# Gates of a Mamba layer's kernel by the silu table in two visits a chunk, and smaller pieces of matrix work between the scan's steps

## The chip, the cores and the metric

One core of a Trainium2 chip runs the program. The metric is the device time of one execution in microseconds (us); the times shown are the median, the lowest and the highest of several executions. A core has a matrix engine (TensorE, "PE" in the profile, with its weight loads as "PEld"), a vector engine (VectorE, "DVE"), a scalar engine (ScalarE, "ACT"), a general one (GpSimd, "POOL") and a queue engine that issues transfers (SyncE, "SP"). Each engine takes its own instructions in order; they meet at semaphores.

## What is computed

The input is x of 4 sequences, 2048 rows each, 256 wide. Two residual layers follow, in float32:

```python
x = x + mamba(layernorm(x));  x = x + ffn(layernorm(x))

# mamba: D_INNER = 512, 16 states
xp, res = split(x @ W_in.T)
xc = silu(conv4(xp) + conv_b)                      # 4 taps along the sequence
B, C, dt = split(xc @ W_x.T)                       # 16, 16 and 1 columns
dt = softplus(dt @ W_dt.T + b_dt)
h = exp(A * dt) * h + dt * B * xc                  # a recurrence over the rows, 512 x 16 states
y = silu(einsum(h, C) + D * xc + res)
return y @ W_out.T

# ffn: ternary weights, 1024 hidden
h = silu(w1(x) * s1) * (w2(x) * s2)
h = gelu(h1(h) * t1);  h = gelu(h2(h) * t2);  return w3(h) * s3
```

## The kernel before

The first part of the program runs over 32 chunks of 256 rows (T = 256). Per chunk it makes the recurrence for 16 states, one state a step, n = 0 to 15, and between these steps all engines do pieces of other stages on other chunks. While the scan works on chunk c, stage `norm` is at chunk c+2, `front` (projection, convolution, gate of the convolution, dt, B and C) at c+1, `post` (gate of y, output projection, residual) at c-1, and `mlp` (first two layers of the feed-forward part, up to the product with h1) at c-1, c-2 and c-3. A second part, from about 2222 us on, makes the other two layers of the feed-forward part over 16 blocks. The change leaves that part as it is.

A step of the scan, on every engine:
- ACT makes two decays (L1028, exp of a chunk's dt times A, 128x510, half of the channels each) into one of three banks of PSUM, so it can be at most three decays ahead of the scan, and copies the last column of an earlier state (`carry`, L1000).
- POOL makes `ub` (L767, L768), two buffers.
- DVE runs two scans (L1165) for state n+1, then adds state n's turned rows, times C, to `acc` (L1178, twice).
- PE turns the state with transposes (L1453), four for each half q of the rows, once the scans are done and DVE has added the same half of the state before. DVE's two additions for n come after the scans for n+1, so PE has about one step for them.

The places of everything else are a table written out by hand: `PE_AT`, `DVE_AT`, `ACT_AT`, `POOL_AT`, `SP_AT`. PE and ACT have 32 places a chunk (place 2n after the first half of step n, place 2n+1 after the second), DVE has 48, POOL and SP 16. A place of `mlp` of 32 and over on PE and ACT lies in a later chunk's body (place 54 is place 22, step 11, one body later). Results of PE's jobs go to three work banks (RA = 3) handed out in the order of the jobs; a job's first piece waits until the bank's last reader is done, and all that PE has behind it waits too.

Gates before: silu(v) is v times (0.5 tanh(0.5 v) + 0.5), as tanh lies in one table set with exp.
- Convolution: ACT copies the bank to `xc` with its bias (L908, four), takes tanh (L915) and a scaled copy (L917) over 128x1024, POOL multiplies (L724).
- y: ACT tanh (L956) and scaled copy (L958) of `acc`, POOL multiplies (L777) into `g`.
- Feed-forward: eight blocks of 128x256 in four pairs. ACT takes tanh of uu (L983), DVE makes (tanh + 1) times uu (L1142, once a pair, frees the bank), then times gg (L1150, twice a pair); ACT rounds to `act_high` (L990), POOL makes the rest (L791), PE multiplies with h1 (L1441).
- softplus: ACT copies dt to `z` (L927, four), takes Abs (L933), Relu (L935) and exp (L937) of 128x1024, then the logarithm (L860).
- Logarithms of softplus and of both layer norms come together in `with_logs`, between two table loads (L865, L876).

Of the kernel before, what the change touches and what calls it, by code (L numbers as in the profile page):

```python
# [31 lines left out]
P = 128  # L32
# [7 lines left out]
def program(nc, x, w_in, conv_w, conv_b, w_x, w_dt, b_dt, a_log, d_skip, w_out,  # L40
# [26 lines left out]
    with ExitStack() as ctx:  # L67
# [11 lines left out]
        half_s1 = sb("half_s1", [P, KH])  # L79
        gate_scale = sb("gate_scale", [P, KH])  # L80
# [74 lines left out]
        tanh1 = sb("tanh1", [P, 2, 2, T], where=a_only)  # L155
        wide1 = sb("wide1", [P, 2, 2, T], where=a_only)
# [65 lines left out]
        scales_ready = sem("scales_ready")  # L222
# [33 lines left out]
        gate_step = sem("gate_step")  # L256
# [11 lines left out]
        tanh_ready = sem("tanh_ready")  # L268
# [9 lines left out]
        def after(eng, s, value):  # L278

            if not (isinstance(value, int) and value <= 0):  # L280
# [6 lines left out]
            norm={25: ('xn',), 27: ('xp0',), 31: ('xp1',)},  # L287
            front={1: ('conv0.a',), 3: ('conv0.b',), 5: ('conv1.a', 'conv1.b'), 14: ('ssm',), 15: ('dtc',), 21: ('acc0',), 25: ('acc1',)},
            post={8: ('gT0',), 11: ('gT1',), 16: ('out.a',), 18: ('out.b',)},
            mlp={28: ('yn',), 39: ('uu0.a',), 40: ('uu0.b',), 45: ('gg0.a', 'gg0.b'), 46: ('uu1.a', 'uu1.b'), 47: ('gg1.a', 'gg1.b'), 49: ('uu2.a', 'uu2.b'), 51: ('gg2.a', 'gg2.b'), 53: ('uu3.a', 'uu3.b'), 56: ('gg3.a',), 57: ('gg3.b',), 63: ('h0.a', 'h0.b'), 65: ('h0.c',), 71: ('h0.d',), 73: ('h1.a', 'h1.b'), 76: ('h1.c', 'h1.d'), 87: ('h2.a', 'h2.b'), 88: ('h2.c',), 89: ('h2.d',), 92: ('h3.a',), 93: ('h3.b',), 95: ('h3.c', 'h3.d')})  # L290
        DVE_AT = dict(low2=44, up=(68, 71, 79, 85), gated=(69, 72, 79, 86))
        ACT_AT = dict(sums=8, x1=22, sums2=25, logs=26, xn=29, xp=(2, 4), conv=(10, 10), silu=13, ssm=17, z=20, soft=21, acc=(26, 30), gate=5, gT=14, high2=32, tanh=(46, 47, 48, 50, 55, 56, 56, 59), high=(49, 53, 58, 61), z_out=(75, 80, 93, 101), a_dt=31)
        POOL_AT = dict(gate=4, silu=7, normalize=14, normalize2=14, dt=14, u=15, low=(25, 27, 29, 31))
        SP_AT = dict(x=0, x1=7, res=15, write_b=7, b=(9, 12, 2, 4), z_out=(35, 41, 46, 47))

        LAST_PIECE = {"uu0": "b", "uu1": "b", "uu2": "b", "uu3": "b", "gg0": "b", "gg1": "b", "gg2": "b", "gg3": "b",
                      "conv0": "b", "conv1": "b", "out": "b", "h0": "d", "h1": "d", "h2": "d", "h3": "d"}
        MLP_BODIES = 4
        PE_STEPS, DVE_STEPS, ACT_STEPS = 2 * NS, 3 * NS, 2 * NS
# [1294 lines left out]
```

## Time and profile before

| what | us |
|---|---|
| median of 3 executions | 2822.73 |
| lowest, highest | 2822.26, 2822.75 |
| the profiled execution, its time | 2821.17 |
| its span, first to last instruction | 2819.5 |
| PE busy | 2623.1 (93%) |
| DVE busy | 2349.9 (83%) |
| ACT busy | 1944.3 (69%) |
| POOL busy | 1840.3 (65%) |

The mean granted clock of TensorE was 0.983 of full speed. Shares of the whole span mix two parts: DVE and POOL are busy almost only in the first. So the table of busy time by stage, the interval from one chunk to the next, and the starts of neighbouring instructions in the timeline say more than the page's shares. In a timeline the duration shown runs a little into the next instruction on the same engine; the distance between two starts is what an instruction takes of its engine's time.

### The profile page before, as it was taken

Reading aid. Unit: us, or ns where it says so; the run is one execution under the profiler, and the core shown is the slowest. Engines: PE = TensorE matmul, PEld = TensorE weight load, DVE = VectorE, ACT = ScalarE, POOL = GpSimd, SP = SyncE. Lnnn points to the kernel's source line nnn. Section 1 sums busy time; section 2 is a strip of 40 time slices with the busy share of each in tenths; the row PEclk is TensorE's granted clock in tenths of the full one; section 3 lists DMA queues with packets and bytes.
Section 4 is the critical chain, followed back from the end, with each engine's and each line's share of the span. In section 5 each row is a group of like instructions: output and inputs, shape, how many; then the busy total and the mean of one; then the engine's idle time right before and its main releaser. Section 6 shows DMA issues by size and latency. Waiting matters only on the chain.

```text
span 2819.5 us, 49137 instructions
## 1 busy us (share of the span) xinstructions
PE 2623.1 (93%) x17154; PEld 2337.7 (83%) x17154; DVE 2349.9 (83%) x3053; ACT 1944.3 (69%) x4040; POOL 1840.3 (65%) x1546
## 2 busy tenths in 40 slices
PE   6678999999999999999999999999978999999998
PEld 4557888888888888888888888888868888888887
DVE  4899999999999999999999999999985455555554
ACT  6888888888888888888888888888866322222221
POOL 3788888888888888888888888888874000000000
PEclk8789999999999999999999999999989999999999
DMA  6111122121221221112112121121132322222211
GB/s 227 42 42 46 57 63 67 57 70 60 61 68 58 64 62 58 58 60 70 57 62 68 57 72 58 61 65 58 54 128 68 114 81 90 83 83 90 90 61 31
DMA packets 130154, 198.78 MB, mean 71 GB/s; under 512 B 16368, under 2 KB 93296, under 8 KB 129904
## 3 DMA queue, kind: packets, MB, share of 16 engines
q1 hardware_dynamic: 129904, 195.57, 21.9%
q8 instruction: 141, 2.31, 0.4%
q14 instruction: 109, 0.89, 0.1%
HBM read 144.68 MB, written 50.86 MB: 69 GB/s over the span
## 4 chain that ended last, share of the span: by engine, by line
PE 49%; ACT 21%; DVE 15%; issue 9%; DMA 1%; POOL 0%; DVEq 0%; ACTq 0%; SPq 0%; POOLq 0%
PE banks L1479 17%; PE banks L1441 9%; DVE h L1165 8%; PE banks L1453 6%; DVE acc L1178 5%; ACT banks L1028 5%; PE banks L1491 4%; PE banks L1357 4%; PE banks L1341 4%; PE banks L1379 2%; ACT act_high L990 2%; PE banks L1427 2%; ACT g L927 1%; ACT L865 1%; ACT L876 1%
## 5 line engine op out<-in xcount | busy, mean ns | idle before, releaser
L1165 DVE TENSOR_TENSOR_SCAN h<-banks,ub 128x512 f32<-128x512 f32 x1024 | 1203.2, 1209 | 75.5 <-ACT banks L1028 61.3
L768 POOL TENSOR_TENSOR ub<-u,b_row 128x1020 f32<-128x1020 f32 x512 | 1215.4, 2374 | 0.1
L1028 ACT ACTIVATE banks<-dt,neg_a 128x510 f32<-128x510 f32 x1024 | 695.0, 684 | 59.0 <-DVE h L1165 59.0
L1178 DVE SCALAR_TENSOR_TENSOR acc<-banks,c_tok,acc 128x512 f32<-128x512 f32 x1024 | 712.6, 738 | 9.6 <-issue 5.1
L1453 PE MATMUL banks<-ident,h 128*128 128x128 f32 x4096 | 580.5, 276 | 71.8 <-DVE acc L1178 69.6
L1453 PEld LDWEIGHTS banks<-ident,h 128*128 128x128 f32 x4096 | 478.4, 143 | 119.4 <-DVE h L1165 68.0
L1441 PE MATMUL banks<-act_high,h_rounded 128*128 128x256 f32 x2048 | 525.0, 294 | 13.3 <-ACT z_out L805 9.0
L1441 PE MATMUL banks<-act_low,h_rounded 128*128 128x256 f32 x2048 | 499.3, 282 | 0.0
L1441 PEld LDWEIGHTS banks<-act_high,h_rounded 128*128 128x128 f32 x2048 | 389.7, 190 | 14.2 <-ACT z_out L805 9.3
L1479 PE MATMUL banks<-act_high,h_rounded 128*128 128x512 f32 x1024 | 398.9, 390 | 0.0
L1479 PE MATMUL banks<-act_low,h_rounded 128*128 128x512 f32 x1024 | 398.9, 390 | 0.0
L1441 PEld LDWEIGHTS banks<-act_low,h_rounded 128*128 128x128 f32 x2048 | 391.0, 191 | 0.0
L1066 ACT ACTIVATE wide<-banks,scales 128x512 f32<-128x512 f32 x128 | 88.1, 688 | 408.2 <-PE banks L1479 408.2
L1427 PE MATMUL banks<-xT_high,w_rounded 128*128 128x256 f32 x1024 | 277.3, 302 | 23.1 <-ACT acc L805 18.8
L1241 DVE CAST act_high<-wide 128x512 fp32r<-128x512 f32 x128 | 54.1, 423 | 263.9 <-PE banks L1491 236.2
L1427 PE MATMUL banks<-xT_low,w_rounded 128*128 128x256 f32 x1024 | 254.7, 280 | 0.0
L1357 PE MATMUL banks<-xp,conv_diag 128*128 128x256 f32 x1024 | 238.0, 380 | 0.0
L791 POOL TENSOR_TENSOR act_low<-wide,act_high 128x512 fp32r<-128x512 f32 x128 | 164.3, 1284 | 110.5 <-ACT act_high L990 110.5
L767 POOL TENSOR_TENSOR ub<-b_u,enter 128x4 f32<-128x4 f32 x512 | 104.6, 204 | 195.8 <-DVE h L1165 187.1
L1479 PEld LDWEIGHTS banks<-act_high,h_rounded 128*128 128x128 f32 x1024 | 192.2, 188 | 40.3 <-issue 0.3
L1479 PEld LDWEIGHTS banks<-act_low,h_rounded 128*128 128x128 f32 x1024 | 192.3, 188 | 39.5
L1427 PEld LDWEIGHTS banks<-xT_high,w_rounded 128*128 128x128 f32 x1024 | 193.0, 188 | 36.2 <-ACT acc L805 24.4
(126 smaller groups left out, 4287.6 us busy)
## 6 DMA issues: line engine op xcount, KB each, us to landing
b_row<-b_scratch SPq DMA_DIRECT2D x128, 512.0 KB, 4.3
z_scratch<-z_out SPq DMA_DIRECT2D x128, 256.0 KB, 3.5
zl<-z_scratch SPq DMA_DIRECT2D x32, 1024.0 KB, 8.0
x_sb<-in_x SPq DMA_DIRECT2D x32, 256.0 KB, 3.1
x_res<-in_x SPq DMA_DIRECT2D x32, 256.0 KB, 4.9
h_full<-in_h SPq DMA_DIRECT2D x2, 4096.0 KB, 16.5
x_scratch<-x_sb SPq DMA_DIRECT2D x32, 256.0 KB, 2.2
xr<-x_scratch SPq DMA_DIRECT2D x16, 512.0 KB, 4.8
```

The lines of the kernel that those rows point to most:

```text
L768: nc.gpsimd.tensor_tensor(ub[:, n % 2, :, 1:], u[:, :, 1:], b_row[:, n // QUARTER % 2, n % QUARTER:n % QUARTER + 1, 1:].to_broadcast([P, E ...
L791: nc.gpsimd.tensor_tensor(act1_low[:, c % 2, 2 * p:2 * p + 2], wide1[:, p % 2], act1_high[:, c % 2, 2 * p:2 * p + 2].bitcast(F32), ALU.sub ...
L1028: nc.scalar.activation(decay_half(k)[:, :, 1:], dt[:, par, 2 * i:2 * i + 2, 1:], ACT.Exp, scale=neg_a[:, n:n + 1]).then_inc(decay_ready, 1)
L1165: nc.vector.tensor_tensor_scan(h[:, n % 2, 2 * i:2 * i + 2].rearrange("p e t -> p (e t)"), banks[:, k % DECAYS, :], ub[:, n % 2, 2 * i:2 * ...
L1178: nc.vector.scalar_tensor_tensor(out=acc[:, par, q], in0=turned[q], scalar=c_tok[:, par, q, n:n + 1], in1=acc[:, par, q], op0=ALU.mult, op ...
L1341: last = nc.tensor.matmul(into[:, i * T:(i + 1) * T], w_in_sb[:, d, e * P:(e + 1) * P], xnT[:, d], start=(d == 0), stop=(d == KD - 1))
L1357: last = nc.tensor.matmul(into[:, i * T:(i + 1) * T], conv_diag[:, e, tap], xp[:, e, tap:tap + T], start=(tap == 0), stop=(tap == TAPS - 1))
L1427: last = nc.tensor.matmul(into[:, i * T:(i + 1) * T], weights[:, d, o * P:(o + 1) * P], rows[:, d], start=(d == 0 and rows is xT_high), st ...
L1441: last = nc.tensor.matmul(into[:, i * T:(i + 1) * T], rounded["h1"][:, k, o * P:(o + 1) * P], rows[:, c % 2, k], start=(k == 0 and rows is ...
L1453: last = nc.tensor.transpose(turned[q][:, e * P:(e + 1) * P], h[:, n % 2, e, q * P:(q + 1) * P], ident[:])
L1479: last = nc.tensor.matmul(into, rounded["h2"][:, k, o * P:(o + 1) * P], part[:, k], start=(k + i == 0), stop=(k == KH - 1 and i == 1))
L1491: last = nc.tensor.matmul(into[:, i * DIM:(i + 1) * DIM], part[:, k, q * P:(q + 1) * P], rounded["w3"][:, k], start=(k == 0 and part is ac ...
```

## The change

- Silu of the convolution, of y and of the feed-forward gate is taken by the silu table, straight out of the banks for convolution and uu, in place for `acc`. POOL's two products, DVE's L1142, the scaled copies and tanh go. DVE's other product (two a pair) stays, with s2 itself as its scale; `silu1` has room for all four pairs.
- ACT visits the silu set twice a chunk: at place 10 for the four convolution blocks of the next chunk and the gate of y of the chunk before, at place 26 for all eight uu blocks. Each visit loads the silu set first and the set with log and exp after. The logarithms need no loads of their own any more, and `with_logs` goes.
- softplus takes Abs and Relu out of the bank, four instructions of 128x256 each, in place of four copies and one instruction each.
- PE's pieces are cut finer (convolution in quarters, `ssm`, `xp`, `acc`, `out` in parts), and the places of nearly everything are new.
- The gelu rows for the second part's first block come one body later.

```diff
         PE_AT = dict(
-            front={1: ('conv0.a',), 3: ('conv0.b',), 5: ('conv1.a', 'conv1.b'), 14: ('ssm',), 15: ('dtc',), 21: ('acc0',), 25: ('acc1',)},
+            front={0: ('conv0.a',), 2: ('conv0.b', 'conv0.c'), 3: ('conv0.d', 'conv1.a'), 5: ('conv1.b', 'conv1.c', 'conv1.d'), 11: ('ssm.a', 'ssm.b'), 13: ('dtc',), 23: ('acc0.a', 'acc0.b', 'acc0.c'), 25: ('acc1.a', 'acc1.b'), 26: ('acc1.c',)},
+            post={12: ('gT0',), 13: ('gT1',), 14: ('out.a',), 15: ('out.b',), 17: ('out.c', 'out.d')},
+            mlp={32: ('yn',), 51: ('uu0.a',), 52: ('uu0.b', 'uu1.a'), 53: ('uu1.b',), 54: ('uu2.a', 'uu2.b', 'uu3.a', 'uu3.b', 'gg0.a'), 57: ('gg0.b', 'gg1.a'), 58: ('gg1.b',), 59: ('gg2.a', 'gg2.b', 'gg3.a'), 61: ('gg3.b',), 71: ('h0.a', 'h0.b', 'h0.c', 'h0.d'), 72: ('h1.a',), 73: ('h1.b',), 74: ('h1.c', 'h1.d'), 79: ('h2.a',), 80: ('h2.b', 'h2.c', 'h2.d'), 81: ('h3.a',), 83: ('h3.b', 'h3.c', 'h3.d')})
-        DVE_AT = dict(low2=44, up=(68, 71, 79, 85), gated=(69, 72, 79, 86))
+        DVE_AT = dict(low2=56, gated=(87, 88, 89, 93))
...
+            def silu_conv(c):
+                for j in range(2):
+                    wait_full(act, f"conv{j}", c)
+                    for i in range(2):
+                        e = 2 * j + i
+                        last = nc.scalar.activation(xc[:, e], bank(f"conv{j}", c)[:, i * T:(i + 1) * T], ACT.Silu, bias=conv_b_sb[:, e:e + 1])
+                    last.then_inc(freed(f"conv{j}", c), 1)
...
+                nc.scalar.activation(acc[:, c % 2], acc[:, c % 2], ACT.Silu).then_inc(g_ready, 1)
...
+                for i in range(2):
+                    o = 2 * p + i
+                    last = nc.scalar.activation(silu1[:, p, i], bank(f"uu{p}", c)[:, i * T:(i + 1) * T], ACT.Silu, scale=scales[:, 0, o:o + 1])
+                last.then_inc(freed(f"uu{p}", c), 1)
...
-                    if s == DVE_AT["up"][p]:
-                        pair = tanh1[:, p % 2].rearrange("p i t -> p (i t)")
-                        nc.vector.scalar_tensor_tensor(out=pair, in0=pair, scalar=1.0, in1=bank(f"uu{p}", c),
-                                                       op0=ALU.add, op1=ALU.mult).then_inc(freed(f"uu{p}", c), 1)
```

ACT around step 13 of a chunk, before (carry and decays are the scan's own; sig, log_var and rstd the logarithms and roots):

```order
L1000 ACTIVATE carry<-h,keep 128x4
L1028 ACTIVATE banks<-dt,neg_a 128x2x255
L990 ACTIVATE act_high<-wide 128x512
L865 ACT_TABLE_LOAD
L860 ACTIVATE sig<-sig 128x1024
L824 ACTIVATE log_var<-row_square,eps 128x2
L852 ACTIVATE log_var<-row_square,eps 128x2
L828 ACTIVATE rstd<-log_var 128x2
L856 ACTIVATE rstd<-log_var 128x2
L876 ACT_TABLE_LOAD
L805 ACTIVATE acc<-banks 128x512
L1028 ACTIVATE banks<-dt,neg_a 128x2x255
```

and the same step after the change (L1008 is the decay, L980 the carry):

```order
L980 ACTIVATE carry<-h,keep 128x4
L1008 ACTIVATE banks<-dt,neg_a 128x2x255
L966 ACT_TABLE_LOAD
L953 ACTIVATE silu<-banks,scales 128x256 x8
L974 ACT_TABLE_LOAD
L1008 ACTIVATE banks<-dt,neg_a 128x2x255
```

Two loads and eight gates now stand between two decays, where two loads, one large and four tiny instructions and a copy stood. A like visit, with four convolution blocks and the gate of y, stands at step 5.

DVE around the gates of the feed-forward part, before (tanh is the product that goes, wide the one that stays):

```order
L1142 SCALAR_TENSOR_TENSOR tanh<-tanh,banks 128x512
L1165 SCALAR_TENSOR_TENSOR h<-banks,ub 128x512
L1150 SCALAR_TENSOR_TENSOR wide<-banks,gate_scale,tanh 128x256 x2
L1165 SCALAR_TENSOR_TENSOR h<-banks,ub 128x512
L1178 SCALAR_TENSOR_TENSOR acc<-banks,c_tok,acc 128x512 x2
```

and after, at steps 13 and 14 (L1137 is the scan, L1150 now the addition, L1122 the product):

```order
L1137 SCALAR_TENSOR_TENSOR h<-banks,ub 128x512 [waits carry_ready,turn_full1,decay_ready,turn_full0,ub_ready]
L1122 SCALAR_TENSOR_TENSOR silu<-banks,scales,silu 128x256 [waits job_full,bank_free0]
L1122 SCALAR_TENSOR_TENSOR silu<-banks,scales,silu 128x256
L1137 SCALAR_TENSOR_TENSOR h<-banks,ub 128x512 [waits decay_ready]
L1122 SCALAR_TENSOR_TENSOR silu<-banks,scales,silu 128x256 [waits job_full,bank_free1]
L1122 SCALAR_TENSOR_TENSOR silu<-banks,scales,silu 128x256
L1150 SCALAR_TENSOR_TENSOR acc<-banks,c_tok,acc 128x512 [waits y_added0,turn_full0]
L1150 SCALAR_TENSOR_TENSOR acc<-banks,c_tok,acc 128x512 [waits y_added1,turn_full1]
```

The four products are one a pair less, and stand closer together, behind ACT's second visit.

## Rows read from the trace of the kernel before

**Rows 1.** The page, part 1: busy us (share of the span) xinstructions.

```profile
PE 2623.1 (93%) x17154; PEld 2337.7 (83%) x17154; DVE 2349.9 (83%) x3053; ACT 1944.3 (69%) x4040; POOL 1840.3 (65%) x1546
```

**Rows 2.** Busy us by stage: PE, PEld, DVE, ACT, POOL; then granted clock, DMA share, GB/s.

```profile
70.00:135.00 65.00, 43.60 (x221) 34.48 (x222) 58.55 (x66) 55.93 (x113) 51.87 (x44) 0.81 0.11 38
...
1000.00:1500.00 500.00, 477.65 (x3367) 432.48 (x3367) 485.64 (x590) 413.21 (x892) 442.92 (x370) 1.00 0.20 63
...
2140.00:2200.00 60.00, 53.03 (x404) 51.33 (x405) 26.32 (x45) 27.59 (x56) 11.40 (x10) 0.95 0.22 75
```

**Rows 3.** One instruction a chunk, L733: ns min/median/max, first and last start.

```profile
L733 POOL TENSOR_TENSOR a_dt<-dt,neg_a x32: 318/328/368, 42.2 to 2064.8; 128x64 f32<-128x64 f32 x32
```

**Rows 4.** Timeline of DVE, 1020 to 1087 us: start, duration, instruction, [idle before it].

```profile
1026.42 0.68 DVE L1134 TENSOR_TENSOR xT_low<-banks,xT_high 128x512 fp32r<-128x512 f32 x1
1027.08 1.41 DVE L1178 SCALAR_TENSOR_TENSOR acc<-banks,c_tok,acc 128x512 f32<-128x512 f32 x2
...
1034.80 2.33 DVE L1165 TENSOR_TENSOR_SCAN h<-banks,ub 128x512 f32<-128x512 f32 x2
1037.05 1.38 DVE L1178 SCALAR_TENSOR_TENSOR acc<-banks,c_tok,acc 128x512 f32<-128x512 f32 x2
1038.35 2.33 DVE L1165 TENSOR_TENSOR_SCAN h<-banks,ub 128x512 f32<-128x512 f32 x2
...
1056.08 0.68 DVE L1142 SCALAR_TENSOR_TENSOR tanh<-tanh,banks 128x512 f32<-128x512 f32 x1
1056.67 1.22 DVE L1165 TENSOR_TENSOR_SCAN h<-banks,ub 128x512 f32<-128x512 f32 x1
1057.80 0.85 DVE L1150 SCALAR_TENSOR_TENSOR wide<-banks,gate_scale,tanh 128x256 f32<-128x256 f32 x2
1058.57 1.21 DVE L1165 TENSOR_TENSOR_SCAN h<-banks,ub 128x512 f32<-128x512 f32 x1
...
1080.69 1.22 DVE L1165 TENSOR_TENSOR_SCAN h<-banks,ub 128x512 f32<-128x512 f32 x1 [1.38 <-ACT banks L1028]
```

**Rows 5.** Waits of DVE in two chunks, 1000 to 1131 us: us, times, longest.

```profile
DVE h L1165 <- ACT banks L1028: 2.8, 2, 1.4
DVE h L1165 <- POOL ub L768: 0.6, 3, 0.2
```

**Rows 6.** The page, part 5: busy, mean ns of one, idle before it and its releaser.

```profile
L768 POOL TENSOR_TENSOR ub<-u,b_row 128x1020 f32<-128x1020 f32 x512 | 1215.4, 2374 | 0.1
...
L791 POOL TENSOR_TENSOR act_low<-wide,act_high 128x512 fp32r<-128x512 f32 x128 | 164.3, 1284 | 110.5 <-ACT act_high L990 110.5
```

**Rows 7.** Timeline of ACT, 1020 to 1087 us.

```profile
1034.57 1.05 ACT L956 ACTIVATE gsig<-acc 128x1024 f32<-128x1024 f32 x1
...
1062.14 1.92 ACT L927 ACTIVATE g<-banks,b_dt_sb,w_dt_sb 128x256 f32<-128x256 f32 x4
...
1071.20 0.85 ACT L983 ACTIVATE tanh<-banks,half_s 128x256 f32<-128x256 f32 x2
1071.91 0.72 ACT L1028 ACTIVATE banks<-dt,neg_a 128x510 f32<-128x510 f32 x1
1072.52 0.23 ACT L844 ACTIVATE minus_mean<-row_sum 128x2 f32<-128x2 f32 x1
...
1074.58 0.61 ACT L990 ACTIVATE act_high<-wide 128x512 fp32r<-128x512 f32 x1
1075.21 1.28 ACT L865 ACT_TABLE_LOAD   x1
1076.51 1.06 ACT L860 ACTIVATE sig<-sig 128x1024 f32<-128x1024 f32 x1
```

**Rows 8.** The chain that ended last, in order of time: PE's stretch without a gap.

```profile
1017.53 1.82 PE banks L1379 x4
1019.34 0.89 PE banks L1381 x8
...
1020.67 0.87 PE banks L1453 x8
...
1023.85 0.93 PE banks L1441 x8
...
1034.76 1.73 PE banks L1357 x8
```

**Rows 9.** Timeline of PE, 2130 to 2232 us, after the last scans.

```profile
2141.11 1.09 PE L1453 MATMUL banks<-ident,h 128*128 128x128 f32 x4 [3.10 <-DVE acc L1178]
```

**Rows 10.** The chain again, at the end of the first part.

```profile
2140.24 0.74 DVE acc L1178
...
2222.61 7.53 PE banks L1479 x33
```

More of the change, by code:

```diff
@@ L296, in program @@
-        LAST_PIECE = {"uu0": "b", "uu1": "b", "uu2": "b", "uu3": "b", "gg0": "b", "gg1": "b", "gg2": "b", "gg3": "b",
-                      "conv0": "b", "conv1": "b", "out": "b", "h0": "d", "h1": "d", "h2": "d", "h3": "d"}
+            norm={28: ('xn',), 29: ('xp0.a', 'xp0.b'), 30: ('xp1.a',), 31: ('xp1.b',)},
+            front={0: ('conv0.a',), 2: ('conv0.b', 'conv0.c'), 3: ('conv0.d', 'conv1.a'), 5: ('conv1.b', 'conv1.c', 'conv1.d'), 11: ('ssm.a', 'ssm.b'), 13: ('dtc',), 23: ('acc0.a', 'acc0.b', 'acc0.c'), 25: ('acc1.a', 'acc1.b'), 26: ('acc1.c',)},
@@ L396, in decay_half, with bodies @@
             return banks[:, k % DECAYS, :].rearrange("p (e t) -> p e t", t=T)
-        def bodies(norm, front, scan, post, mlp, start, steps):
+        def bodies(norm, front, scan, post, mlp, start, steps, also=lambda c, n: None):
             def body(c):
@@ L412, in between @@
                         norm(to_norm, n)
+                    also(c, n)
                 scan(c, between)
@@ L449, in program @@
         W3_AFTER = 3
-        FIRST_ROWS = [(CHUNKS + 1, 4 * o) for o in range(KH)]
+        FIRST_ROWS = [(CHUNKS + 2, 2 * o) for o in range(KH)]
         e_place = {}
@@ L926, in front @@
+                    after(act, dt_ready, c)
                     for e in range(ET):
[L927 to L935 removed]
+                        last = nc.scalar.activation(soft[:, e], rows[:, 0:T], ACT.Abs, scale=w_dt_sb[:, e:e + 1], bias=b_dt_sb[:, e:e + 1])
@@ L936, in front @@
+                    last.then_inc(soft_step, 1)
+                if n == ACT_AT["z"] + 1:
+                    rows = bank("dtc", c)
+                    after(act, scan_done, 2 * NS * (c - 1))
+                    for e in range(ET):
+                        last = nc.scalar.activation(dt[:, par, e], rows[:, 0:T], ACT.Relu, scale=w_dt_sb[:, e:e + 1], bias=b_dt_sb[:, e:e + 1])
+                    last.then_inc(freed("dtc", c), 1)
+                if n == ACT_AT["z"] + 2:
                     act.wait_ge(soft_step, 3 * c + 1)
@@ L949, in post @@
             def post(c, n):
-                if n == ACT_AT["gate"]:
-                    for q in range(NT):
-                        act.wait_ge(y_added[q], NS * (c + 1))
-                    if c >= 1:
-                        wait_full(act, "out", c - 1)
-                    gs = gsig[:].rearrange("p n d -> p (n d)")
-                    nc.scalar.activation(gsig[:], acc[:, c % 2], ACT.Tanh, scale=0.5).then_inc(gate_step, 1)
-                    act.wait_ge(gate_step, 2 * c + 1)
-                    nc.scalar.activation(gs, gs, ACT.Copy, scale=0.5, bias=0.5).then_inc(gate_step, 1)
                 if n == ACT_AT["x1"]:
@@ L1046, in scan @@
                     between(2 * n + 1)
-            bodies(norm, front, scan, post, mlp, lambda: None, ACT_STEPS)
+            bodies(norm, front, scan, post, mlp, lambda: None, ACT_STEPS, silus)
             def first(blk, o):
@@ L1387, in post @@
                     job, part = (piece.split(".") + [""])[:2]
-                    into = bank(job, c) if part == "b" else wait_bank(job, c)
+                    into = wait_bank(job, c) if part in ("", "a") else bank(job, c)
                     if job.startswith("gT"):
```

261 lines of the change are left out of this document (116 added, 145 removed).

## The prediction

> **What bounds the kernel now.** I read the page's busy shares first [rows 1]: PE 93%, DVE 83% of the span. [...] The second part begins near 2222 us and is not touched. L733 runs once a chunk [rows 3]: (2064.8 - 42.2) / 31 = 65.25 us a chunk. So what counts is the chunk's period.
>
> DVE's timeline [rows 4] gives that period as a sum of distances between starts. A plain step is two scans, 2.25 us, and two additions, 1.30: 3.55. Sixteen are 56.8. The product that goes, L1142, takes 1056.67 - 1056.08 = 0.59, four are 2.4. The pair of L1150 takes 1058.57 - 1057.80 = 0.77, four are 3.1. L1134 takes 0.66. Sum 62.9. The remaining 2.3 us are waits and their restarts: 1.4 a chunk for a decay while ACT sits between its two table loads, 0.3 for POOL's `ub` [rows 4, 5], the rest some 0.1 at each restart. DVE bounds the first part, and PE is only 4% behind it.
>
> **DVE: less work.** L1142 goes: 65.25 - 2.3 - 2.4 = **60.6 us a chunk** without waits. If all waits stayed as they are it would be 62.9.
>
> **POOL: less work.** Two products of 128x1024 go (L724, L777; L768 with 1020 elements takes 2.37 us [rows 6]). POOL was busy 442.9 of 500 us, 57.8 a chunk, and falls to about 53. That pays only through the 0.3 us of waits.
>
> **ACT: the same work, in larger lumps.** Gone per chunk: tanh and scaled copy twice, 4 x 1.0 (L956) [rows 7]; large Abs and Relu, 2 x 1.0; four copies L927, 1.8. Added: gate of y 1.0; Abs and Relu as 8 x 0.45 = 3.6 (1.92 for four L927, which they resemble); two table loads, 2 x 1.3. So 7.8 go and 7.2 come. Silu itself is in no executed row. Tanh of 128x256 takes 0.71 / 2 = 0.36 (L983 to L1028) [rows 7], exp of 510 columns 0.61, L927 with two operands per partition 0.45; I take 0.36, with 0.45 as the upper bound and 0.36 as the lower.
>
> Each load takes 1.28, and the instruction behind it starts 1.30 after the load's start [rows 7]. Nothing else shows around the load. [...]
>
> The visits then are: step 5, 1.3 + 4 x 0.36 + 1.0 + 1.3 = 5.0 us without a decay; step 13, 1.3 + 8 x 0.36 + 1.3 = 5.5 us. Before, the longest lump was 1.3 + 1.0 + 0.7 + 1.3, and it cost DVE 1.4. ACT may be three decays ahead. It can issue decay 26 when the scans of step 11 end, call that 0: carry 0.2, decay 0.6, visit 5.5, decay 27 0.6: ready at 6.9. DVE wants decay 27 after two additions, two scans, two additions and one scan: 1.3 + 2.25 + 1.3 + 1.1 = 6.0. **0.9 us is lost, and 0.5 more if ACT comes late** (the copy of h3 and a norm stand just ahead), unless DVE waits for something else there. At step 5 the same sum gives 6.4 against 6.0 + 0.66 for L1134, which now stands in that stretch: nothing lost.
>
> **PE: the same work, otherwise placed.** Prices from the chain [rows 8]: four transposes 0.44; eight f32r products with h1 0.93, a uu or gg half 0.47; a 256-column f32 product 0.43 (two records); `acc` 1.82 + 0.89. PE's work a chunk adds to some 61.5 us and doesn't change. Its spread does. In the new places, with 0.87 of transposes a step, the steps carry, in us:
>
> 1: 4.3 (convolution), 2: 3.5, 3: 4.6 (h0 whole), 4: 2.8, 5: 4.5, 6: 2.4, 7: 4.0, 8: 6.8 (h2, h3.a, half of `out`), 9: 4.1 (h3), 10: 2.3, 11: 5.9 (uu2, uu3, gg0.a, `acc0`).
>
> That is 45.2 us in eleven steps, and DVE's eleven steps with L1134 are 39.7. PE starts this stretch 0.7 us behind DVE's scans of step 1 (it waits for DVE's addition) and DVE needs the last transposes of step 11 one step and 0.65 later. Without waits DVE is there 11 x 3.55 + 0.66 + 0.65 = 40.4 us after the start; PE is there after 0.7 + 45.2 - 2.7 (`acc0` stands behind) + 0.2 = 43.4. **DVE must wait 3.0 us**, spread over the additions of steps 8 to 11. In the other five steps PE has 16 us of work against DVE's 21 and stands idle; it can't use that, as its pieces wait for results of that time.
>
> The two losses don't add. DVE's 3.0 us in steps 8 to 11 give ACT time: decay 27 is then ready at about the moment when DVE asks. PE's own wait for uu0's bank (uu3 takes it, and it is freed by the first pair of the visit) is covered too, as PE comes to uu3 about a microsecond behind that. Small waits (additions of steps 12 and 15, one product for gg2) I put at 0.5. L791, which PE's h0 waits for, just fits: POOL makes four of them in steps 1 to 4, where it has 3.7 us of work a step.
>
> **Sum.** 60.6 + 3.0 + 0.5 = 64.1, say **64.2 us a chunk, 1.0 less than before**. In the first three chunks the pipeline isn't full, DVE is busy 58.6 of 65 us and the clock is down at 0.81 [rows 2]; I count nothing there. About 28 chunks gain 28 us.
>
> **The end of the first part** gets longer. It is 82 us now from DVE's last addition to the second part [rows 10]. After the last scans PE is already idle 7 of 60 us [rows 2], with a gap of 3.1 us and transposes at half speed behind it (0.44 becomes 0.74 and more) [rows 9]. In the new places all uu and gg of a chunk stand behind the chunk before's h products, so nothing covers the way from gg3 over product 0.8, `act_high` 0.6 and two L791 of 1.28 each [rows 6] to h0: 4 us exposed in each of two bodies, some of which was exposed before. I take +6, bounds 0 and +12. The profiled execution goes from 2821.2 to 2799; the median was 1.6 above it: **2800**.
>
> **Rivals.**
> 1. *PE's stretch is no bound.* If the steps overlap better than the sum of pieces, PE drops out and ACT's visit at step 13 decides: 60.6 + 1.4 + 0.5 + 0.4 = 62.9 a chunk, 28 x 2.3 = 64 less, +6: about 2764. For it: PE shows 22 us idle in 500 now [rows 2]. Against: the chain's prices are distances in a dense stretch.
> 2. *Slower: the visits decide.* ACT copies banks for PE in order (h2, h3, `out`) and comes to its visit late whenever PE is late; then the visit's 5.5 us stand behind PE's 3.0 instead of under them, and PE's uu3 waits for its bank with all transposes behind it. Speaking for it is that my sum leaves ACT almost no slack at decay 27, and that silu at 0.45 would lengthen the visit by 0.7. It decides from 1.1 us more at step 13; all of it would be 60.6 + 3.5 + 1.9 = 66.0, 28 x 0.8 + 6 more: about 2851.
> 3. *Nothing left.* PE's backlog grows by the small restarts that I left out, one us a chunk: 65.2, about 2824 with a mild end.
> [...]
>
> **How the numbers follow.** Forecast 0.52, rival 1 0.20, rival 2 0.13, rival 3 0.13, rival 4 0.02. The forecast's own range is 63.6 to 64.9 a chunk: 2783 to 2820. For 8 in 10 the range leaves out rivals 2 and 4 and the lower fringe of rival 1: 2762 to 2826. A measurement of this kernel tells 0.2%, 5.6 us, from no change. Faster: rival 1 and nearly all of the forecast, 0.71. Same: rival 3 mostly, 0.13. Slower: 0.16.
>
> **What would show it.** In the profile after, L733's successor should repeat every 64.2 us. DVE's waits should name PE's transposes (additions of steps 8 to 11) with about 3 us a chunk, where none stood, and the wait for decays should fall under 0.5. PE should have no idle from step 1 to 11 and 2 us behind. The silu rows should be 0.36 apart and the loads 1.28 with nothing behind them. After the last scans the drain should be 6 us longer than 82. [...] I'm wrong altogether if the period stays at 65 with DVE waiting less than 2.

## The result and the profile after

The changed kernel takes **2812.56 us** (median of 7, 2811.11 to 2815.1) against 2822.75 (7 executions, 2821.21 to 2825.33): a ratio of 0.9965, 95% interval 0.9953 to 0.9976. It is faster by 10 us, less than half of the 22.7 that were forecast. Its profiled span is 2810.7 us against 2819.5, and its mean granted clock 0.974 against 0.983.

The page, part 1, beside [rows 1]; then busy time by stage, beside [rows 2] (the third stage is not the same piece of work, as the first part ends 8 us earlier); then the line that starts once a chunk, beside [rows 3]:

```profile
PE 2619.4 (93%) x17154; PEld 2338.5 (83%) x17154; DVE 2284.3 (81%) x2923; ACT 1947.2 (69%) x4070; POOL 1696.1 (60%) x1483
```

```profile
70.00:135.00 65.00, 43.39 (x231) 34.90 (x230) 60.45 (x68) 54.73 (x114) 48.85 (x42) 0.83 0.11 38
1000.00:1500.00 500.00, 478.87 (x3373) 433.70 (x3372) 474.19 (x566) 413.06 (x895) 409.60 (x356) 0.99 0.20 62
2140.00:2200.00 60.00, 48.77 (x373) 47.27 (x372) 14.28 (x25) 28.49 (x56) 11.92 (x10) 0.93 0.10 36
```

```profile
L721 POOL TENSOR_TENSOR a_dt<-dt,neg_a x32: 319/331/1297, 34.2 to 2042.8; 128x64 f32<-128x64 f32 x32
```

Line numbers have moved: L1137 is the scan, L1150 the addition, L1122 the product, L1008 the decay, L1434 the state's transposes, L1422 the products with h1, L774 POOL's subtraction. The starts of that once-a-chunk line split the time of the profiled executions into stretches that can be added up:

| stretch | before | after | difference |
|---|---|---|---|
| start to the first a_dt | 42.2 | 34.2 | -8.0 |
| four chunks to the fifth a_dt | 262.7 | 257.0 | -5.6 |
| the next 26 chunks | 26 x 65.23 | 26 x 64.84 | -10.0 |
| one more | 64.1 | 65.7 | +1.6 |
| last a_dt to the second part | 157.8 | 172.0 | +14.2 |
| second part | 596.9 | 595.9 | -1.0 |

The surprise is inside the third line. The 26 intervals have two values: **16 are 64.3 us, which is the forecast's 64.2, and 10 are 65.7.** Before they were all 65.2. But for the first, the long ones are two and three chunks apart in turn. Two kernels of the experiments below with the same chunks (the one that waits for the scales and the one that moves h2 and h3 at the end) show the same order, the former shifted by a chunk.

In a chunk of either kind the waits are those of the forecast. Timeline of DVE (start, duration, instruction, idle before it), the additions of steps 8, 9 and 10, and of ACT, the visit at step 13:

```profile
1051.47 0.75 DVE L1150 SCALAR_TENSOR_TENSOR acc<-banks,c_tok,acc 128x512 f32<-128x512 f32 x1 [0.75 <-PE banks L1434]
...
1055.01 1.41 DVE L1150 SCALAR_TENSOR_TENSOR acc<-banks,c_tok,acc 128x512 f32<-128x512 f32 x2 [0.54 <-PE banks L1434]
...
1059.16 0.75 DVE L1150 SCALAR_TENSOR_TENSOR acc<-banks,c_tok,acc 128x512 f32<-128x512 f32 x1 [0.50 <-PE banks L1434]
1060.54 0.75 DVE L1150 SCALAR_TENSOR_TENSOR acc<-banks,c_tok,acc 128x512 f32<-128x512 f32 x1 [0.63 <-PE banks L1434]
```

```profile
1059.79 1.28 ACT L966 ACT_TABLE_LOAD   x1
1061.08 3.08 ACT L953 ACTIVATE silu<-banks,scales 128x256 f32<-128x256 f32 x8
1064.17 1.28 ACT L974 ACT_TABLE_LOAD   x1
1065.47 0.69 ACT L1008 ACTIVATE banks<-dt,neg_a 128x510 f32<-128x510 f32 x1
```

DVE waits 2.4 us a chunk for PE where it waited for nothing, and no more than 0.3 for decays where it waited 1.4 [rows 4]. Eight silus take 3.1 us, 0.38 apart, and behind each load the next instruction starts within 0.02 us of its end.

What differs between the two kinds of chunk is the clock behind PE's one gap, the wait for the first scan of a chunk. Timeline of PE in a long chunk and in the next, short one:

```profile
1016.94 0.90 PE L1434 MATMUL banks<-ident,h 128*128 128x128 f32 x4 [2.22 <-DVE h L1137]
1017.63 1.06 PE L1398 MATMUL banks<-ident,xn 128*128 128x128 f32 x4
1018.49 1.92 PE L1331 MATMUL banks<-xp,conv_diag 128*128 128x256 f32 x4
```

```profile
1082.66 0.65 PE L1434 MATMUL banks<-ident,h 128*128 128x128 f32 x4 [2.22 <-DVE h L1137]
1083.15 0.60 PE L1398 MATMUL banks<-ident,xn 128*128 128x128 f32 x4
1083.59 1.03 PE L1331 MATMUL banks<-xp,conv_diag 128*128 128x256 f32 x4
```

Busy time in the same places; the number behind the last bracket is the granted clock:

```profile
1014.50:1017.00 2.50, 0.28 (x3) 0.06 (x2) 2.50 (x4) 2.25 (x5) 0.48 (x2) 1.00 0.00 0
1017.00:1018.50 1.50, 1.50 (x9) 1.50 (x10) 1.50 (x2) 0.80 (x2) 1.50 (x2) 0.57 0.00 0
1018.50:1020.50 2.00, 2.00 (x7) 1.53 (x7) 1.25 (x2) 1.77 (x4) 2.00 (x2) 0.50 0.00 0
```

```profile
1082.50:1084.00 1.50, 1.34 (x10) 1.32 (x11) 1.50 (x3) 1.23 (x3) 1.32 (x2) 1.00 0.00 0
```

The gap is the same 2.22 us. In the long chunk the clock then stands at 0.50 for 3.4 us: four convolution products take 1.92 us instead of 1.03, the transposes come late (eight at 1020.19, 1.25 us), and the second addition of step 0 starts 1.4 us late; the profile names no releaser for it:

```profile
1021.10 0.75 DVE L1150 SCALAR_TENSOR_TENSOR acc<-banks,c_tok,acc 128x512 f32<-128x512 f32 x1 [1.35 <-issue]
```

That is the whole difference of 65.7 - 64.3. Before, no such fall stood between 260 and 2075 us (mean granted clock 1.00).

### The profile page after: what moved, and what is told of

It is laid out like the page before. It is cut to its first block and busy times, and to the rows that moved or that the text cites. A ratio compares the mean times of both kernels' runs of the same rounds, so it can differ in the third digit from the quotient of the medians.

```text
span 2810.7 us, 48687 instructions
## 1 busy us (share of the span) xinstructions
PE 2619.4 (93%) x17154; PEld 2338.5 (83%) x17154; DVE 2284.3 (81%) x2923; ACT 1947.2 (69%) x4070; POOL 1696.1 (60%) x1483
## 5 line engine op out<-in xcount | busy, mean ns | idle before, releaser
L1137 DVE TENSOR_TENSOR_SCAN h<-banks,ub 128x512 f32<-128x512 f32 x1024 | 1200.9, 1206 | 39.2 <-ACT banks L1008 23.7
L1150 DVE SCALAR_TENSOR_TENSOR acc<-banks,c_tok,acc 128x512 f32<-128x512 f32 x1024 | 723.0, 736 | 95.3 <-PE banks L1434 76.4
L1434 PE MATMUL banks<-ident,h 128*128 128x128 f32 x4096 | 613.5, 280 | 149.8 <-DVE acc L1150 75.1
L1008 ACT ACTIVATE banks<-dt,neg_a 128x510 f32<-128x510 f32 x1024 | 692.1, 683 | 59.5 <-DVE h L1137 55.5
L1434 PEld LDWEIGHTS banks<-ident,h 128*128 128x128 f32 x4096 | 489.5, 144 | 240.4 <-DVE h L1137 165.8
L1422 PE MATMUL banks<-act_high,h_rounded 128*128 128x256 f32 x2048 | 516.7, 292 | 11.8 <-POOL act_low L774 11.8
L1422 PE MATMUL banks<-act_low,h_rounded 128*128 128x256 f32 x2048 | 495.6, 281 | 0.0
L1422 PEld LDWEIGHTS banks<-act_high,h_rounded 128*128 128x128 f32 x2048 | 389.6, 190 | 14.2 <-issue 12.5
L1422 PEld LDWEIGHTS banks<-act_low,h_rounded 128*128 128x128 f32 x2048 | 390.8, 191 | 0.1
L1408 PE MATMUL banks<-xT_high,w_rounded 128*128 128x256 f32 x1024 | 270.5, 298 | 2.5 <-ACT silu L953 2.4
L1331 PE MATMUL banks<-xp,conv_diag 128*128 128x256 f32 x1024 | 252.9, 391 | 0.0
L1331 PEld LDWEIGHTS banks<-xp,conv_diag 128*128 128x128 f32 x1024 | 191.2, 197 | 22.5
```

Of the source, the lines that this page charges most:

```text
L1008: nc.scalar.activation(decay_half(k)[:, :, 1:], dt[:, par, 2 * i:2 * i + 2, 1:], ACT.Exp, scale=neg_a[:, n:n + 1]).then_inc(decay_ready, 1)
L1137: nc.vector.tensor_tensor_scan(h[:, n % 2, 2 * i:2 * i + 2].rearrange("p e t -> p (e t)"), banks[:, k % DECAYS, :], ub[:, n % 2, 2 * i:2 * ...
L1150: nc.vector.scalar_tensor_tensor(out=acc[:, par, q], in0=turned[q], scalar=c_tok[:, par, q, n:n + 1], in1=acc[:, par, q], op0=ALU.mult, op ...
L1331: last = nc.tensor.matmul(into[:, i * T:(i + 1) * T], conv_diag[:, e, tap], xp[:, e, tap:tap + T], start=(tap == 0), stop=(tap == TAPS - 1))
L1408: last = nc.tensor.matmul(into[:, i * T:(i + 1) * T], weights[:, d, o * P:(o + 1) * P], rows[:, d], start=(d == 0 and rows is xT_high), st ...
L1422: last = nc.tensor.matmul(into[:, i * T:(i + 1) * T], rounded["h1"][:, k, o * P:(o + 1) * P], rows[:, c % 2, k], start=(k == 0 and rows is ...
```

## The experiments

### Does the clock behind the gap cost the missing time?

The first kernel gives PE five useless products at the turn, into a bank that is rewritten next:

```diff
+                if 3 <= c < CHUNKS - 1:
+                    into = wait_bank("yn", c - 2)
+                    for k in range(5):
+                        nc.tensor.matmul(into[:, 0:T], ident[:], w_in_sb[:, 0, 0:T], start=True, stop=True)
```

> The changed kernel, and PE makes five useless products of ident with a part of w_in (256 columns, 0.43 us each) into yn's bank while it waits for the first scans of a chunk (chunks 3 to 30); nothing else moves. Theory (a chunk takes 64.28 us, and in 10 of 26 chunks 1.44 more, as the granted clock falls to half behind PE's gap of 2.2 us at the chunk's turn): no half-clock stretch between 320 and 2000 us, every period 64.3, 2812.6 - 11 x 1.44 = 2797, ratio to the kernel before 0.991. Rival (the long chunks come from a transfer or another wait, and the clock is only seen beside it): periods of 65.7 stay in about 10 chunks, 2812.

Measured: 2795.7 us (4 executions, 2794.52 to 2796.5), ratio 0.990 (0.9882 to 0.9918). All chunks from the fourth on take 64.3 us (64.28 to 64.51), and no long one is left:

```profile
L721 POOL TENSOR_TENSOR a_dt<-dt,neg_a x32: 322/329/1295, 34.7 to 2027.0; 128x64 f32<-128x64 f32 x32
```

More work on the busiest engine made the kernel 17 us faster. The cause of the long chunks is shown: from the fifth to the last a_dt it is 1736.0 us instead of 1751.6, so the eleven falls in it cost 15.5 us, 1.4 each.

### Where do the 8 us at the start come from?

```diff
+                if c == 0:
+                    act.wait_ge(scales_in, 16 * 5)
```

> The changed kernel, and ACT waits for the scales' loads before the first chunk's convolution gates, as the kernel before did there. Theory (8 us of the gain by the first a_dt came from that wait, which went with half_s1): the first a_dt moves from 34.2 us back to about 42, and the total to 2812.6 + 8 = 2820. Rival (the finer pieces of PE and the shorter chain of gates made the start faster): first a_dt within 1.5 us of 34.2, total 2812 to 2814.

Measured: 2813.47 us (4 executions), and the first a_dt at 34.0 as without the wait. The theory, a wait for the scales, fell. The rows tell where the 8 us are. PE and POOL before, then PE and POOL after:

```profile
26.46 3.65 PE L1366 MATMUL banks<-xc,w_x_sb 128*128 128x256 f32 x8 [4.51 <-DVE xc L1208]
```

```profile
39.64 2.57 POOL L717 TENSOR_SCALAR xn<-x_sb,minus_mean,rstd 128x256 f32<-128x256 f32 x2 [31.79 <-ACT rstd L828]
```

```profile
23.38 1.97 PE L1342 MATMUL banks<-xc,w_x_sb 128*128 128x256 f32 x8 [1.02 <-ACT xc L938]
```

```profile
34.19 1.30 POOL L721 TENSOR_TENSOR a_dt<-dt,neg_a 128x64 f32<-128x64 f32 x1 [13.94 <-DVE dt L1181]
```

The gate of the convolution is ready 3.1 us earlier (23.38 against 26.46), without tanh, copy and DVE's product. PE's next products take 1.7 us less, at full clock. From there to softplus is 1.5 us less, as the load that stood in it is gone. And POOL's layer norm of the second chunk, which stood 1.7 us in front of a_dt because its logarithm came with softplus, is made at 19 us. That adds up to 8.0. The clock's share was put to the test with two more loads in chunk 0:

```diff
                 for j in range(2):
+                    if c == 0 and j == 1:
+                        nc.scalar.preload_act_table_set("gelu_and_others")
+                        nc.scalar.preload_act_table_set("silu_and_others")
```

> The kernel with the five useless products, and in chunk 0 alone two more table loads (2.6 us) between the two halves of the convolution's silu. Before the change TensorE waited 4.51 us for the input of w_x's products and these took 3.65 us at half clock; after it the wait was 1.02 and they took 1.97. Theory, that the clock is a term of the 8 us gained at the start: with the wait back at about 3.6 us the products take 3.65 again, and the first a_dt comes 2.6 + 1.7 = 4.3 later, at 38.9. Rival, that only the length of the chain of gates counts: they stay at 1.97 and the first a_dt comes at 37.2.

Measured (one execution): the wait grew to 2.28 us only, yet the products fell to half clock again (mean granted clock 0.55 from 25.7 to 29.3 us), and the first a_dt came at 38.1, 3.4 later than in the kernel it is built on. The clock's 1.5 us (3.48 against 1.97) are among them, at a smaller gap than I had asked for; the time lies between the theory's 38.9 and the rival's 37.2, and the products alone tell them apart:

```profile
25.75 3.48 PE L1345 MATMUL banks<-xc,w_x_sb 128*128 128x256 f32 x8 [2.28 <-ACT xc L941]
```

### Is it PE's dense stretch that makes DVE wait?

The third kernel moves h3 behind the stretch (in the changed kernel, without the useless products):

```diff
-            mlp={..., 81: ('h3.a',), 83: ('h3.b', 'h3.c', 'h3.d')})
+            mlp={..., 95: ('h3.a', 'h3.b', 'h3.c', 'h3.d')})
```

with xp1.b, the copy and the store of h3 moved to fit.

> The changed kernel with h3's four quarters (3.7 us of PE) moved from steps 8 and 9 to the last place of step 15, xp1.b one place up, and the copy and store of h3 behind it. Theory (PE's dense stretch holds DVE by 3 us a chunk, and PE's gap at the turn lets the clock fall): both go at once. DVE's waits for transposes fall under 0.5 us a chunk, ACT's visit at step 13 decides and DVE waits 1 to 1.5 us for decays, no half-clock stretch, period 62.5 to 63; 2812.6 - 26 x (64.84 - 62.8) = 2760, ratio 0.978. Rival (DVE's waits come from the order and the shared banks, not from PE's load): period stays over 64, ratio over 0.99.

Measured: 2818.7 us (10 executions), ratio 0.9986 (0.9976 to 0.9996), 6 us slower than the changed kernel. From the fifth a_dt on all chunks take 64.75 us (64.7 to 65.0), without a fall of the clock; the 6 us lie behind the last a_dt, where 775.4 us follow instead of 767.9. The expectation fell, and the period and the ratio are those of its rival. The waits of DVE over 500 us, and of PE:

```profile
DVE acc L1150 <- PE banks L1434: 21.8, 22, 1.4
```

```profile
PE banks L1408 <- ACT silu L953: 7.3, 7, 1.0
```

DVE still waits 2.8 us a chunk, at other additions, one of them the first of the chunk. PE came earlier to uu3, whose bank the visit at step 13 has not freed yet, and waits there 1.0 a chunk with the transposes behind it. The gap at the turn was filled with real work and the clock held, but h3 takes 3.7 us in a gap of 2.2, which, as I read it, pushed the transposes behind it.

So I took work away, to see how far PE's amount is the bound. On the kernel with useless products:

```diff
+                        parts = (act1_high,) if p >= 2 and 3 <= c < CHUNKS - 3 else (act1_high, act1_low)
                         for k in range(first_k, first_k + KH // 2):
-                            for rows in (act1_high, act1_low):
+                            for rows in parts:
```

> The kernel with the five useless products, without the low halves of the products for h2 and h3 in chunks 3 to 28 (32 products of 0.118 us, 3.8 us of TensorE's work a chunk, steps 7 to 9 of its dense stretch); that part of the computation is left out. My theory: TensorE's stretch binds now, and with 3.8 us less the visit at step 13 does: VectorE's waits for transposes at steps 8 to 11 fall under 0.5, in their place stands a wait of 0.9 to 1.4 for decay 27, and the period falls from 64.28 to 62.9 as in the first rival's sum; time about 2795.7 - 26 x 1.4 = 2759. Rival, that VectorE's own time and latencies between engines set the period: it stays over 64.0, time over 2788. A third, that nothing waits for ScalarE: 61.5 to 62, about 2730.

Measured: 2789.13 us (2 executions, 2785.77 and 2792.49). Most chunks take 63.57 us, some 64.1 to 65.4 around seven places where the clock fell again. So 3.8 us less on PE give 0.7 a chunk, half of the 1.4 that I expected. By its time alone the rival's "over 2788" would fit too, but the two executions are 6.7 us apart, and the period is not over 64.0. The next bound is a wait of PE, and DVE's behind it:

```profile
1050.82 0.38 PE L1408 MATMUL banks<-xT_high,w_rounded 128*128 128x256 f32 x1 [1.74 <-ACT silu L953]
```

```profile
1052.96 0.75 DVE L1150 SCALAR_TENSOR_TENSOR acc<-banks,c_tok,acc 128x512 f32<-128x512 f32 x1 [2.05 <-PE banks L1439]
```

The visit decides, as the first rival had it for a PE that is no bound, but not through decay 27: through the bank that its first pair frees late. That costs 0.7 us more than the 62.9 of that rival.

The other side is more work on DVE, in the shadow of PE's stretch and outside it, four products of two SBUF tensors each:

```diff
+                    if 3 <= c < CHUNKS - 1 and 5 <= n <= 8:      # the other kernel: n >= 12
+                        nc.vector.tensor_tensor(spare[:], w_in_sb[:, 0, 0:512], w_in_sb[:, 1, 0:512], ALU.mult)
```

> The kernel with the five useless products at the turn (every chunk 64.28 us, second part from 2198.7), and in 28 chunks VectorE gets four more products of 128x512, one behind the additions of each of steps 5 to 8, where TensorE's work is dense and VectorE later waits 2.2 us for its transposes. Each should take some 0.6 us, 2.4 a chunk; the result is thrown away. My theory, that TensorE's dense stretch from step 1 to 11 sets the time there: the products lie in the waits, the period grows by no more than 0.3 us, VectorE's waits for transposes fall from 2.4 to under 0.5 a chunk; time under 2805. Rival, that VectorE's own work sets it and its waits are mere phase: the period grows by 2.4 us to 66.7, time about 2863.

> The same kernel with the same four products behind the additions of steps 12 to 15, behind the last of VectorE's waits for TensorE. My theory: nothing covers them there, since TensorE stands idle and waits for VectorE at the turn. The period grows by the whole of the products, about 2.4 us to 66.7, time about 2863. Rival, that the chunk's total of work on TensorE (some 61.9 of 64.3 us) sets the period wherever VectorE works: TensorE would use nothing of the later start, so its wait at the turn grows from nothing to 2.4 us or, where it has a backlog, the period grows by less than 1 us: under 2824.

Measured: 2957.4 us and 70.04 a chunk for the early ones, 2983.45 and 70.74 for the late ones (71.7 to 71.8 in five chunks; in these kernels the clock fell 12 and 21 times, behind waits of PE of 1.9 and of 2.4 to 3.1 us, mostly without making the chunk longer). Both expectations missed, because one product takes 1.94 us and not 0.6:

```profile
L1168 DVE TENSOR_TENSOR spare<-w_in_sb 128x512 f32<-128x512 f32 x28 | 54.4, 1942 | 0.0
```

Of the early ones each takes 1.87 us of DVE's time from start to start, 7.5 in all, and 1.7 of that were absorbed; of the late ones 1.63, 6.5 in all, and 0.1. The direction is that of the theory. I repeated the comparison with three products that read a bank and one SBUF tensor, at steps 5 to 7 and at 12 to 14; they take 0.74 us, 0.66 from start to start:

```diff
+                        if q == 1 and 3 <= c < CHUNKS - 1 and 5 <= n <= 7:      # the other kernel: 12 <= n <= 14
+                            nc.vector.scalar_tensor_tensor(out=spare[:], in0=turned[q], scalar=c_tok[:, par, q, n:n + 1], in1=acc[:, par, q],
+                                                           op0=ALU.mult, op1=ALU.add).then_inc(spare_done, 1)
```

> The comparison of the extra products again, with products that read a bank and one tensor in SBUF, as the addition L1150 does (0.74 us), since the ones with two SBUF inputs took 1.94: three more on VectorE in steps 5 to 7, 2.2 us a chunk, on the kernel with the five useless products at the turn. Theory (VectorE has 2.4 us of waits for TensorE behind steps 5 to 7 that can take them): the extra work goes into the waits, the period is 64.3 to 64.6 and the waits for transposes fall from 2.4 to under 0.8 a chunk; under 2806. Rival (the waits follow VectorE's phase and don't shrink): 66.5, about 2857.

> The same three products in steps 12 to 14, behind VectorE's waits. Theory: 64.28 + 2.2 = 66.5 us a chunk, the waits for transposes at steps 7 to 11 stay at 2.4; about 2857. Rival (TensorE's whole chunk is the bound and works off a backlog in steps 12 to 15): under 65.0, under 2816.

Measured: 2823.71 us and 65.17 a chunk early, 2850.96 and 66.16 late. Late, 1.9 of the 2.0 us are paid and DVE's waits stay; early, 0.9 is paid, more than the 0.3 I allowed. The waits of DVE in 500 us, early and late:

```profile
DVE acc L1158 <- PE banks L1446: 11.3, 21, 0.6
```

```profile
DVE acc L1158 <- PE banks L1446: 19.3, 32, 0.8
```

and PE's, in the kernel with the early products:

```profile
1046.07 0.63 PE L1446 MATMUL banks<-ident,h 128*128 128x128 f32 x4 [0.64 <-DVE acc L1158]
```

The wait at step 8 is gone, those at steps 9 and 10 remain. At steps 5 to 7 PE is only just behind DVE: pushed by the products, DVE makes PE wait 0.64, and the later part of the stretch moves with it. So what binds is the part from step 8 on (h2, h3 and `out`), not eleven steps as one sum.

### What does one more load cost?

```diff
+                    if visit == 1 and 3 <= c < CHUNKS - 1:
+                        nc.scalar.preload_act_table_set("gelu_and_others")
                     nc.scalar.preload_act_table_set("silu_and_others")
```

> The kernel with the five useless products, and one more table load (of a set that is not used) at the head of the visit at step 13 in 28 chunks. Theory: a load costs ScalarE 1.28 us and nothing behind it, and there is no slack at decay 27 (it ends just as VectorE asks for it), so VectorE waits 1.3 us there in each chunk: period 65.5 to 65.6, time about 2831. [...] Rival 1, that the waits for TensorE still leave slack: period grows by under 0.3, under 2804.

Measured: period 65.53, as forecast to 0.1 us, in an execution of 2830.79 us; the median of five is 2836.09. ACT at the visit, and DVE behind it:

```profile
1067.67 1.28 ACT L967 ACT_TABLE_LOAD   x1
1068.96 1.28 ACT L968 ACT_TABLE_LOAD   x1
1070.25 3.02 ACT L953 ACTIVATE silu<-banks,scales 128x256 f32<-128x256 f32 x8
```

```profile
1073.29 0.75 DVE L1152 SCALAR_TENSOR_TENSOR acc<-banks,c_tok,acc 128x512 f32<-128x512 f32 x1 [1.24 <-PE banks L1440]
```

A load costs 1.28 us, the period grew by 1.25, and the path has no slack for it. The way is again not the one I wrote down: DVE waits for transposes of step 11, which stand on PE behind uu3's bank:

```profile
1071.14 0.39 PE L1410 MATMUL banks<-xT_high,w_rounded 128*128 128x256 f32 x1 [0.92 <-ACT silu L953]
```

The bank comes free 0.89 us after the first silu's start here (1070.25). In the kernel without the added load the first silu starts at 1053.71 and PE comes to uu3 at 1054.81, so the slack was 0.2 us. The median of the five executions is 5 us above the 2831 that I expected; only the execution of 2830.79 has a profile, and the other 5 us stay unexplained.

### What makes the end longer?

In chunks 29 and 30 h2 and h3 went behind uu and gg, where they might cover the way to the next h0:

```diff
+        PE_LAST.update({94: ('h2.a', 'h2.b', 'h2.c', 'h2.d'), 95: ('h3.a', 'h3.b', 'h3.c', 'h3.d')})
```

> The changed kernel, and only for the last chunks but one (29 and 30) h2 and h3 stand behind the next chunk's uu and gg, at the end of a body. Theory (the end of the first part is 12 us longer because nothing covers the way from gg3 to h0: two gaps of 5.7 us on PE, and half clock behind each): both gaps fall under 2.5 us, the clock stays full, the second part starts 9 to 13 us earlier; 2812.6 - 10 = 2802, ratio 0.993. Rival (the end is bound by ACT's two table loads and by POOL's four subtractions, wherever PE's work stands): under 3 us gained.

Measured: 2812.4 us (5 executions), no gain. The profiled execution was the slowest, 2817.54 us; in it the second part starts at 2219.2, 174.4 after the last a_dt. The theory fell. PE's waits from 2060 us on went from 11.8 us for L774 to 9.5, and others took their place:

```profile
PE banks L1430 <- POOL act_low L782: 9.5, 3, 4.1
PE banks L1416 <- ACT silu L961: 3.8, 2, 2.3
```

The roundings now queue on ACT behind copies that wait for PE. The end is a chain over all four engines; moving one of its pieces moves the gap. In the changed kernel the gaps look like this (timeline of PE), and the last two have half clock behind them (busy time by stage, the granted clock behind the last bracket); the first lies inside a longer stretch of half clock, from 2123 to 2137:

```profile
2130.96 0.55 PE L1422 MATMUL banks<-act_high,h_rounded 128*128 128x256 f32 x1 [1.88 <-POOL act_low L774]
...
2167.93 0.55 PE L1422 MATMUL banks<-act_high,h_rounded 128*128 128x256 f32 x1 [4.20 <-POOL act_low L774]
...
2197.97 0.55 PE L1422 MATMUL banks<-act_high,h_rounded 128*128 128x256 f32 x1 [5.68 <-POOL act_low L774]
```

```profile
2168.00:2171.50 3.50, 3.50 (x19) 3.50 (x20) 0.00 (x0) 0.00 (x0) 0.00 (x0) 0.58 0.02 5
...
2198.00:2205.00 7.00, 7.00 (x46) 7.00 (x47) 5.57 (x12) 1.21 (x2) 0.00 (x0) 0.74 0.00 0
```

So the gaps stayed, and PE was kept busy in them, on top of the useless products at the turn:

```diff
+                        if p == 0 and part == "a":
+                            for k in range({CHUNKS - 3: 8, CHUNKS - 2: 30, CHUNKS - 1: 40}.get(c, 0)):
+                                nc.tensor.matmul(into[:, 0:T], rounded["h1"][:, 0, 0:P], rounded["h1"][:, 0, 0:T], start=True, stop=True)
```

> The kernel with the five useless products at the turn, and in the end of the first part useless f32r products of 0.118 us in the gap before h0 of the last three chunks: 8, 30 and 40, written to the bank that h0 takes, inside gaps of 1.9, 4.2 and 5.7 us. Theory: behind the two long gaps the clock stood at half for some 3 us each, so h0's products took 0.21 instead of 0.12; with TensorE busy it stays full and the second part starts 2.5 to 4 us earlier than 2198.7: about 2792.5. Rival, that the fall comes whatever TensorE does there, or that the gaps are shorter than the fillers: no gain or a loss of up to 3 us, 2795 to 2799.

Measured: **2792.14 us** (4 executions, 2791.12 to 2793.44), ratio 0.989 (0.9874 to 0.9907), 3.6 below the kernel it is built on and 20 below the changed kernel. It is the fastest kernel that leaves nothing out. The clock stays at 1.00 through the gaps, and from the last a_dt to the second part it is 166.0 us instead of 171.7 (the second part takes 1.7 us longer in this execution, and the medians differ by 3.6 only):

```profile
2147.76 0.39 PE L1425 MATMUL banks<-act_high,h_rounded 128*128 128x256 f32 x1 [0.59 <-POOL act_low L774]
```

Half clock before h0's products is thus some 5.6 of the 14.2 us that the end grew by. The other 8 I read as the exposed way from gg3 to h0, but no run took it away, and half clock isn't ruled out there either: from the last a_dt to the second part it stood for 27 us before, 44 after, 51 with the useless products at the turn and still 34 here (mean granted clocks 0.91, 0.87, 0.85 and 0.90). The second and third of these stretches last 172.0 and 171.7 us, so 7 us more of half clock cost nothing there; not all of it counts.

## Why the prediction fell short

**The sum of a chunk held, its terms less well.** 60.6 + 3.0 + 0.5 gave 64.2, and a chunk at full clock takes 64.28. By distances between starts, a chunk of the kernel with useless products (DVE, 1017.94 to 1082.23 us) is 60.5 of work and 2.7 of waits for PE with their restarts (2.4 without), at the additions named, where I had 3.0; the other 1.1, where I had 0.5, are delays of 0.1 to 0.2 at single scans and additions, most without a named wait. That the two misses cancel in part is luck. Silu at 0.36 measured 0.38, a load 1.28, and the instruction behind it started within 0.02 us of its end. An added load moved the period by 1.25 us.

**The step that failed is the sentence on PE's idle time.** The prediction said that PE "stands idle; it can't use that" in the other five steps and priced it at nothing. A gap of 2.22 us is there as said, and in 10 of 26 chunks TensorE's clock halves behind it, 1.4 us each on DVE's path. With the useless products in the gap the falls are gone and the median is 17 us lower. From the fifth to the last a_dt, 27 chunks, it is then 23.9 us less than before, where 1.0 a chunk was forecast. (That the whole gain is 27 us, close to the forecast's 28 for the chunks alone, is chance: start and end cancel.) The hint was in the rows: transposes at half speed behind a gap of 3.1 us [rows 9]. I used it for the end of the part and not for the turn.

**The start and the first chunks were priced at nothing and gave 13.6.** 8.0 come from the shorter chain of chunk 0, in four terms that add up. 5.6 come from the four chunks to the fifth a_dt, 257.0 us where it was 262.7. 4.0 of them are in the third chunk. As I read it DVE, busy 58.6 of 65 us [rows 2], was the path there too, and loses the same work in it; no run tests that.

**The end was +6 with bounds 0 and 12 and measured +14.2.** The 4 us exposed in each of two bodies were right in kind: the waits are 4.2 and 5.7 (and 1.9). The half clock behind them, 5.6 us, was left out, the same omission as at the turn; the rest of the miss stays open. The starting point was also off: the addition at 2140.24 [rows 10] is not DVE's last (2148.8), so it was 73.8 us from the last addition to the second part and not 82. It grew to 85.8.

**PE's stretch of eleven steps** was right in its total effect and wrong in its extent. Extra work on DVE at steps 5 to 7 is half paid for, not hidden; the waits arise from step 8 on. And with PE relieved the visit at step 13 acts through uu3's bank, a wait that the prediction called "covered", with "about a microsecond" to spare: it is, but by 0.2 us only. PE was also nearer to DVE than the prediction's 4%: its busy time was 8.0 of 500 us lower [rows 2].

**Rivals.** The first (PE no bound, 2764) is refuted by the waits; its sum is not reached even with 3.8 us less on PE. The second (slower) did not come: the visit is on time by 0.2 us, and 1.3 us more in it cost 1.25 a chunk. The third (nothing left, 2824) is nearest in time but not in cause. The fourth, given 0.02, used a term that no run shows; the runs show 1.28 us for a load and 0.02 or less between it and the next instruction.

Set against each other in the profiled executions: -13.6 at the start, +8 at the end, +20 in the chunks, -1 in the second part. Of the 20 the clock is 15.5; the rest is one forecast chunk that the table counts at the start, the last chunk, which took 64.1 before already, and periods of 64.28 and more where 64.2 were forecast. These errors cancel in part; without the gains at the start the miss would have been twice as large.

What stays open is why the clock falls in 10 chunks of 26 with the same gap and the same work before it. The regular order of the falls, and its shift by a chunk in a kernel whose chunks are the same, speak for the moment at which the gap comes and against something in the chunk; no run here separates the two.

## What to carry to other kernels

TensorE's gap of 2.22 us had two prices here, the gap and, in 10 chunks of 26, the half clock behind it, 1.4 us on DVE's path. Where the transposes behind a gap are on the critical path, price both, and try a few useless products in the gap before moving real work into it: here they cost four lines and gave more than the whole change. When two engines' bounds lie within 1 us of each other, taking work off one may give little (3.8 us off PE gave 0.7 here), so look up what is late next, down to the bank that a reader frees, before counting a gain.

## What the runs showed of the hardware

- The clock fell behind a gap of 2.22 us in some chunks and not in others, each time to 0.50 of full speed and for about 3.4 us; in the end of the first part half clock stood for up to 13.7 us at a stretch in the changed kernel and 20.5 in the one with the useless products. With TensorE busy in that gap it never fell in 28 chunks. Where the same useless products stood and another gap was left, it fell behind that in some chunks: behind 1.75 us in the kernel with less work on PE, behind 1.93 with the four early products, behind 2.4 to 3.1 with the four late ones. In the kernel before, the one with the added load and the one with three late products, no wait of PE between 260 and 2020 us was over 1.1 us, and no fall stood there.
- A DVE product of 128x512 took 1.94 us with both inputs in SBUF beside POOL's products of 2.37 us, and 0.74 with one input in a bank. At the start POOL's two normalizations took 2.57 us in the kernel before, beside DVE's `dt` and `u`, products of two SBUF inputs, and 1.10 in the changed kernel, with DVE idle. Behind four of the slow DVE products in a row the next scan started 0.47 to 0.48 us after the end of POOL's product that ran when they started. What made them slow no run separates.
